# A two-layer attention kernel: the first layer's seventh transposed block goes behind the output projection and into the other PSUM bank

## The reference

```python
qkv = (x @ qkv_w.T).reshape(*x.shape[:-1], c, 3 * h)
q, k, v = (qkv[..., :h], qkv[..., h:2 * h], qkv[..., 2 * h:])
aff = jnp.einsum('bmich,bmjch->bmijh', q, k)
gate = jax.nn.sigmoid(x @ gate_w.T + gate_b).reshape(*x.shape[:-1], c, h)
factor = 1.0 / math.sqrt(c)
bias = x2d @ x2d_w.T * factor
weights = jax.nn.softmax(aff + bias[:, None], axis=-2)
out = jnp.einsum('bmrch,bmirh->bmich', v, weights) * gate
out = out.reshape(*x.shape[:-1], c * h) @ final_w.T + final_b
...
x = x + _L0_conv_ref(_gn(x), ...)
x = x + _L1_conv_ref(_gn(x), ..., 16)
```

## Time and profile before

| | |
|---|---|
| median of 3 runs | 3560.49 us (3558.21 to 3562.08) |
| the profiled execution | 3560.76 us |
| its span, first to last instruction | 3558.9 us |
| TensorE busy | 3369.3 us (95%) |
| VectorE busy | 2968.9 us (83%) |
| ScalarE busy | 2753.6 us (77%) |
| GpSimd busy | 2165.3 us (61%) |
| granted TensorE clock, first layer | 1.00 of full speed |

### The profile page before, as it was taken

One profiled execution on the slowest core, in us unless ns is written; L12 is line 12 of the kernel. 1 busy time (PEld: TensorE's weight loads), 2 busy tenths in 40 slices (PEclk: granted clock), 3 DMA queues, 4 the chain that ended last, 5 costly groups with the idle time before them and its releaser, 6 DMA issues.

```text
span 3558.9 us, 123057 instructions
## 1 busy us (share of the span) xinstructions
PE 3369.3 (95%) x36747; PEld 3001.8 (84%) x36747; DVE 2968.9 (83%) x10850; ACT 2753.6 (77%) x8999; POOL 2165.3 (61%) x4107
## 2 busy tenths in 40 slices
PE   4569999999999999999999999799999999999999
PEld 1148888888888888888888887799999999999998
DVE  4569999999999999999999998688888888888886
ACT  1149999999999999999999998567766667766666
POOL 0048888888888888888888886344444444443443
PEclk7579999999999999999999999899999999999999
DMA  9921111111111111111111111111111111111111
GB/s 356 370 91 54 53 48 49 53 50 48 53 53 44 53 53 46 51 53 53 44 53 53 44 53 34 42 51 53 53 53 53 50 50 53 53 53 53 51 49 49
DMA packets 189033, 238.42 MB, mean 67 GB/s; under 512 B 11825, under 2 KB 176177, under 8 KB 184753
## 3 DMA queue, kind: packets, MB, share of 16 engines
q1 hardware_dynamic: 184368, 204.17, 18.2%
q10 hardware_dynamic: 4608, 33.56, 2.5%
HBM read 170.57 MB, written 67.11 MB: 67 GB/s over the span
## 4 chain that ended last, share of the span: by engine, by line
PE 71%; DVE 9%; issue 8%; ACT 6%; DMA 4%; POOL 1%; DVEq 1%; SPq 0%; ACTq 0%; POOLq 0%
PE work L477 26%; PE work L486 11%; PE turn L538 7%; PE score L629 5%; PE score L508 5%; PE mix L662 4%; PE mix L550 4%; DMA x_chunk<-xT 4%; DVE prob L936 3%; ACT prob L734 3%; PE turn L646 3%; PE score L538 2%; ACT xnT L754 2%; PE turn L647 2%; PE turn L648 2%
## 5 line engine op out<-in xcount | busy, mean ns | idle before, releaser
L364 POOL TENSOR_SCALAR prob<-prob,row_inv 128x256 f32<-128x256 f32 x2048 | 1029.0, 522 | 213.0 <-DVE row_inv L942 211.5
L734 ACT ACTIVATE prob<-prob,row_min 128x256 f32<-128x256 f32 x2048 | 1022.0, 508 | 68.0 <-DVE row_min L936 61.4
L477 PE MATMUL work<-src,w 128*128 128x256 f32 x7680 | 1062.7, 287 | 10.3 <-DVE src L925 6.7
L477 PEld LDWEIGHTS work<-src,w 128*128 128x128 f32 x7680 | 946.9, 189 | 12.1 <-DVE src L925 7.4
L415 POOL TENSOR_SCALAR prob<-prob,row_inv 128x160 f32<-128x160 f32 x1024 | 391.1, 401 | 767.8 <-DVE row_inv L1055 767.8
L936 DVE CUSTOM_DVE_ANT_0 prob<-score,neg_bias 128x256 f32<-128x256 f32 x2048 | 756.9, 417 | 48.9 <-PE score L508 46.6
L799 ACT ACTIVATE prob<-prob,row_min 128x160 f32<-128x160 f32 x1024 | 431.2, 426 | 142.7 <-DVE row_min L1048 142.6
L538 PE MATMUL turn<-ident,prob 128*128 128x128 f32 x3072 | 471.9, 276 | 11.4 <-DVE probT L947 2.6
L486 PE MATMUL work<-w,src 128*128 128x256 f32 x3072 | 427.9, 288 | 9.7 <-ACT xnT L754 7.4
L477 PE MATMUL work<-att,wf 128*128 128x256 f32 x3072 | 432.6, 290 | 4.0 <-DVE att L1006 2.6
L538 PEld LDWEIGHTS turn<-ident,prob 128*128 128x128 f32 x3072 | 342.9, 141 | 85.0 <-POOL prob L364 45.3
(11 more groups left out here) (112 smaller groups left out, 6118.5 us busy)
## 6 DMA issues: line engine op xcount, KB each, us to landing
pair_chunk<-pairT ACTq DMA_DIRECT2D x32, 1024.0 KB, 7.7
x_chunk<-xT SPq DMA_DIRECT2D x32, 1024.0 KB, 8.4
x_tok<-x_nat SPq DMA_DIRECT2D x128, 256.0 KB, 3.3
x_sb<-xT SPq DMA_DIRECT2D x128, 256.0 KB, 3.4
x1T<-y_sb SPq DMA_DIRECT2D x128, 256.0 KB, 2.2
x_sb<-x1T SPq DMA_DIRECT2D x128, 256.0 KB, 2.9
outT<-y_sb SPq DMA_DIRECT2D x128, 256.0 KB, 2.2
prob<-w_d SPq DMA_DIRECT2D x1, 1024.0 KB, 8.2
```

The lines of the kernel that those rows point to most:

```text
L364: pool.tensor_scalar(prob[:, h, ib], prob[:, h, ib], row_inv[:, h, ib:ib + 1], 1.0, ALU.mult, ALU.mult).then_inc(norm_done[0], 1)
L477: ins = pe.matmul(out[:, cb], w[:, of_w, kb, cols + cb * P:cols + (cb + 1) * P], x[:, of_x, kb], start=n == 0, stop=n == len(terms) - 1)
L734: act.activation(prob[:, h, ib], prob[:, h, ib], ACT.Exp, bias=row_min[:, h, ib:ib + 1], scale=-1.0, accum_out=row_sum[:, h, ib:ib + 1]).t ...
```

## The change

On TensorE turn 6 moves from ahead of the output projection to behind it, directly ahead of turn 7. Turn 6 now goes to the bank `turn`, turn 7 to `score[:, 0]`. The waits follow the banks: turn 6 waits for copy 5, turn 7 for the next row's first `mins` (which have emptied `score[:, 0]`), turn 0 of the next row for copy 6 instead of copy 7, and `scores(m, 1)` for copy 7 instead of copy 6. On ScalarE copy 6 moves behind four exponentials of the next row. On VectorE copy 7 reads the other bank and keeps its place.

```diff
@@ scores
                     if hg == 0:
                         wait(pe, turn_done[0][1], r.times(PAIRS0, -3))
                     else:
-                        wait(pe, turn_done[0][0], r.times(PAIRS0, 0))
+                        wait(pe, turn_done[0][1], r.times(PAIRS0, 0))
@@ turns
                     to = turn[:]
-                    if h in (1, 6):
+                    if h in (1, 7):
                         to = score[:, 0].rearrange("p b t -> p (b t)")
                     if h == 0:
-                        wait(pe, turn_done[0][1], m.times(PAIRS0, 0))
+                        wait(pe, turn_done[0][0], m.times(PAIRS0, 0))
...
                     elif h == 6:
-                        wait(pe, turn_done[0][1], m.times(PAIRS0, 2))
-                        if nxt.exists:
-                            wait(pe, min_done[0], nxt.times(TB * H0, TB))
-                    else:
                         wait(pe, turn_done[0][1], m.times(PAIRS0, 3))
+                    elif nxt.exists:
+                        wait(pe, min_done[0], nxt.times(TB * H0, TB))
@@ TensorE, body0
                     turns(5)
-                    turns(6)
                 if last.exists:
                     wait(pe, att_done[0], last.times(1, 1))
...
                     project(work[:, 1], wf0, 0, att).then_inc(y_ps[0], 1)
                 if m.exists:
+                    turns(6)
                     turns(7)
@@ ScalarE, body0
-                if m.exists:
-                    turn_copy(6, score[:, 0].rearrange("p b t -> p (b t)"))
                 if nxt.exists:
                     exps(nxt, 0)
                     exps(nxt, 1)
+                if m.exists:
+                    turn_copy(6, turn[:])
+                if nxt.exists:
                     exps(nxt, 2)
@@ VectorE, body0
-                    turn_copy(7, turn[:])
+                    turn_copy(7, score[:, 0].rearrange("p b t -> p (b t)"))
```

## The result

The changed kernel takes 3655.72 us (median of 4 runs, 3654.23 to 3660.19), the kernel before 3559.35 us beside it (3556.26 to 3562.08): a ratio of 1.0271, with an interval of 1.0259 to 1.0283. It is 96 us slower. The forecast was 3585 us, and its range ended at 3655. All of it lies in the first layer: in the two profiled executions the span grew by 93.8 us and the last `att` comes 94 us later. The layer runs from the first `att` to the last from 260.5 to 2240.7 us before and from 263.1 to 2334.7 us now.

A forecast was written before the change was run, and what follows sets the result against it. A ring through TensorE, ScalarE and VectorE's `att` closes in rows b and d; in a and c ScalarE is late. Four rows grow 0.75 us to 63.12, times 32 is 24 us: 3585 us (own range 3576 to 3594; eight-in-ten range 3572 to 3655).

The forecast's parts named there:

- Turn 6 behind the projection: TensorE: idle 0.54 us before the projection; turn 6's 0.43 us lengthens b and d fully, a by 0.23.
- the collision: VectorE's `src` and GpSimd's addition to `g_tok` exclude each other; with the addition first, `src` takes 1.76 instead of 0.70 us.
- the four rows: Rows a, b, c, d of the first layer's loop body, 15.59, 15.08, 16.31, 15.39 us before; forecast 62.97 to 63.28 together.
- Row b: Second of four rows, 15.08 us before: forecast 15.51 if it keeps what makes it shorter than d, otherwise 15.82.
- Copy 6 and row c: ScalarE: copy 6 no longer delays exponentials, VectorE's 0.57 us wait for them goes; row c falls from 16.31 to 15.82 us.
- Banks and waits: The exchanged banks and waits for turns 6, 7, 0 and the scores were taken to cost nothing.
- margin of 0.13 us at `scores(m, 1)`: Row b: copy 7 ends at 1217.35, scores start at 1217.48; taken as nothing, bounds 0 to 0.2 us a row.
- the rival on the source: GpSimd's addition to `g_tok` starts before VectorE's `src`, whose margin was 0.13 us; 3600 to 3655 us, chance 0.27.
- idle time spent at copy 0 instead: ScalarE outside row c: time gained by moving copy 6 is only spent waiting at copy 0 for turn 0.
- The price of the collision: `src` 1.06 us longer when GpSimd's addition is first; in every second row 68 us, hence 3653 us.
- The stall at turn 6: TensorE: if `att_done` came 0.43 us earlier, the change gives back stalls, 29 us, hence 3532; faster, chance 0.09.
- VectorE's order: VectorE bounds a and c: a no longer, c loses 0.72, b and d gain 0.43; 3565 us, no change, chance 0.09.

The follow-up runs named there:

- first experiment: The changed kernel with GpSimd's addition to `g_tok` made to wait for VectorE's low half of `src`: 3583.88 us, ratio 1.0078 to the kernel before.
- fifth experiment: The kernel before with only copy 6 moved behind four exponentials on ScalarE, turn 6 and banks as before: 3569.72 us, ratio 1.0028.
- ninth experiment: The kernel before with copy 6 behind four exponentials, `att`'s cast ahead of copy 4, and GpSimd's addition waiting for `src`: 3577.41 us, ratio 1.0053.
- third experiment: The kernel before with one more small copy (128 x 2) on ScalarE right ahead of the cast of `src`: 3613.36 us, ratio 1.0163.
- fourth: The kernel before with the same small copy (128 x 2) on ScalarE right behind the cast of `src`: 3560.42 us, ratio 1.0013.
- second experiment: The kernel before with GpSimd's addition to `g_tok` made to wait for `src`: 3556.57 us, ratio 1.0003.

## Why the prediction was right in its direction and wrong in its size

*Turn 6 behind the projection: right.* TensorE's idle time ahead of the projection was put at 0.54 us and is 0.57; the projection starts 0.05 us behind `att` in each row; and with the collision out the four rows are 15.82, 15.52, 15.88 and 15.87 us, against the forecast 15.82, 15.51 to 15.82, 15.82 and 15.82. Row b fell at its lower end and kept what makes it shorter, c and d came 0.06 and 0.05 higher. The sum is 63.09 for 63.12; that it fits to 0.03 is luck in part, for the forecast took the middle for b, and b's error and that of c and d cancel. The first experiment's ratio makes it 28 us (21 to 34) over the kernel before, for the forecast's 24.

*Copy 6 and row c: right, with two causes apart.* c was to come to 15.82 and came to 15.88. Copy 6 alone takes some 0.25 of it (16.33 to 16.07). VectorE's inverse waiting for the exponentials is no longer among the larger waits.

*Banks and waits: right,* nothing that shows, by the run with the old banks. The margin of 0.13 us at `scores(m, 1)` held.

*The step that failed* stands in the rival on the source: "So it moves by nearly as much, and the margin shrinks by a part of the 0.13." It shrank by all of it. The earlier trace rows have the addition 0.13 us behind `src` in b; its profile has them together in the changed kernel, in b and d alike. The timelines of ScalarE and PEld tell where the 0.13 went. Before, in b, with the query projection at 1215.48:

```profile
1216.82 0.49 ACT L734 ACTIVATE prob<-prob,row_min 128x256 f32<-128x256 f32 x1
1217.21 0.19 ACT L734 ACTIVATION_READ_ACCUMULATOR prob<-prob,row_min 128x1 f32 x1
1217.31 0.57 ACT L744 CAST nqT<-work 128x512 fp32r<-128x512 f32 x1
...
1219.83 0.42 PEld L538 LDWEIGHTS turn<-ident,prob 128*128 128x128 f32 x4 [0.41 <-POOL prob L364]
```

and in the changed kernel, in d (b has the same distances):

```profile
1229.38 1.48 PEld L477 LDWEIGHTS work<-src,w 128*128 128x128 f32 x12
...
1233.77 0.42 PEld L536 LDWEIGHTS turn<-ident,prob 128*128 128x128 f32 x4 [0.41 <-issue]
...
1230.74 0.21 ACT L732 ACTIVATION_READ_ACCUMULATOR prob<-prob,row_min 128x1 f32 x1
1231.10 0.59 ACT L742 CAST nqT<-work 128x512 fp32r<-128x512 f32 x1
```

From the query projection to turn 0, from where `src` is reached, it is 4.35 us before and 4.39 after; both values occur before the change. From the query projection to the cast of the queries, from where VectorE's scores, the inverse and with it GpSimd's addition are reached, it is 1.83 and 1.72. Before, six exponentials ran up to the cast without a gap and held it up. Now TensorE turns to the queries 0.43 us later, ScalarE is ahead, and the cast starts as soon as the queries are there. So `src` lost 0.15 us against the addition (0.04 + 0.11). Before, the margin was 0.13 in b and 0.12 in d in the stretch of the rows shown, and between 0.06 and 0.19 in the steady rows b and d of the layer. Now it is 0.01 the other way in nearly all of them, of which the cast's gain is the larger part. The prediction named that very cast, put "a little" on it and gave the case 0.27; read to the end, the six exponentials without a gap would have told that the cast had all of the 0.43 to gain from, up to its own readiness. That would have been the place to take the collision as the likeliest.

Nor was turn 6 alone in it. In the fifth experiment, with only copy 6 moved, the cast of b already comes 1.76 us behind the query projection:

```profile
1221.79 1.44 PEld L477 LDWEIGHTS work<-src,w 128*128 128x128 f32 x12
...
1223.55 0.58 ACT L744 CAST nqT<-work 128x512 fp32r<-128x512 f32 x1
```

The margins in b and d are 0.07 and 0.02 us there (medians), for 0.12 in both before. The prediction had put the moved copy at nothing outside c ("idle time spent at copy 0 instead"); by itself it takes 0.05 us of the margin in b and 0.10 in d. No run has turn 6 moved and copy 6 in its old place, so what each of the two takes in the changed kernel isn't divided further.

*The price of the collision: right.* It was put at 1.06 us in every second row, 68 us, for 3653. It is 68 to 72 us between the first experiment and the changed kernel: 0.98 us in d, 1.33 in b, which also loses what made it shorter, and nothing in a and c. There the addition comes some 0.4 to 1.0 us behind `src`, because VectorE's statistics stand ahead of `y_sb` and hold up the inverse. The prediction's own terms, 63.12 and twice 1.06, make 65.24 us for four rows, where 65.4 were measured. So that rival's time was 3 us from the result, and the range's upper end, set at it and not behind it, fell 0.7 us short.

*The stall at turn 6, and VectorE's order:* neither came about. The ninth experiment shows the first in the other direction: when `att` comes earlier, that stall does decide, in every row.

## What to carry to other kernels

When a change delays one of two instructions that exclude each other, write down the margin of their starts in each kind of row and follow both chains back to a common origin, asking on each which engine had been running without a gap; a stretch without a gap is slack that the delay gives to that chain, and the margin moves by it. If the two come within some tenths of a us and one of them is not urgent, let it wait for the other's semaphore: that cost nothing here (1.0003) and was worth about 70 us. And a filler in front of a wait must be ready early itself, or it becomes the wait.

## What the runs showed of the hardware

VectorE's `src` and GpSimd's addition behave as if they shared one lock. If VectorE has it, `src` takes 0.69 us (up to 0.99 where a multiplication of GpSimd was still running) and the addition 1.71 to 1.80; if GpSimd has it, the addition takes 1.28 to 1.30 us and `src` 1.75 to 1.87. The Trainium skill, "SBUF — State Buffer", section "Who interferes with whom", has this, with the order of issue as what decides, and the lengths agree with it. By the recorded starts the order agrees too, but for near ties and for one case.

In the traces of five kernels (before, after, and the third, fourth and fifth experiment) GpSimd won whenever its addition is recorded between 81 ns ahead of `src` and 36 ns behind it (146 cases). In one more, near the layer's start in the third experiment, `src` took 2.24 us with the addition recorded 0.41 us later; there a multiplication of GpSimd was still running when `src` began, and the addition followed it directly, so `src` lost to both. In rows c of the changed kernel the three stand alike, and `src` lost to the multiplication alone (0.96 to 0.99 us); what made the difference is open. Otherwise VectorE won wherever the addition is recorded 46 ns or more behind. In the fifth experiment both stand side by side, VectorE and GpSimd at 789.6 and at 1355.9 us:

```profile
789.61 1.87 DVE L926 TENSOR_TENSOR src<-xnT,src 128x512 fp32r<-128x512 f32 x1 [0.31 <-ACT src L765]
...
789.65 1.29 POOL L380 TENSOR_TENSOR g_tok<-g_tok,gn_row 128x512 f32<-128x512 f32 x1
...
1355.88 0.69 DVE L926 TENSOR_TENSOR src<-xnT,src 128x512 fp32r<-128x512 f32 x1 [0.31 <-ACT src L765]
...
1355.92 1.80 POOL L380 TENSOR_TENSOR g_tok<-g_tok,gn_row 128x512 f32<-128x512 f32 x1
```

Both pairs read 0.04 us apart (36 and 46 ns), with opposite outcomes and 1.2 us between them. So the recorded start is not the moment that decides, and a margin below 0.05 us in VectorE's favour is none for this pair. Between `att` and GpSimd's multiplication the tie lies elsewhere: VectorE won with the multiplication recorded 20 ns ahead (second experiment: `att` 0.70 us, the multiplication 0.99) and once with 48 ns (third), and lost once at 48 ns (changed kernel: 0.97 and 0.48) and always from 52 ns on. What it is that decides was not tried.
